# Offset convolution on whitened images in SBUF, with the row weights made pair by pair beside it

## What is computed

```python
x = _L0_conv_ref(x, L0_conv_beta)                  # X_hat = wm @ (x - mean) + beta
om = conv_general_dilated(x, w_off, padding=1) + b_off      # 27 planes: 9 y offsets, 9 x offsets, 9 mask logits
mask = sigmoid(om[:, 18:])
py = off_y + hs + ky ;  px = off_x + ws + kx       # where each of the 9 taps samples
sampled = bilinear(x, py, px) * mask
out = einsum("bckhw,ock->bohw", sampled, w) + b
out = relu(batch_norm(out)) + x
```

## Time and profile before

| what | us |
|---|---|
| median of three runs | 2315.51 |
| the profiled execution | 2317.37 |
| its span, first to last instruction | 2315.2 |
| busy PE / DVE / ACT / POOL | 1634.0 / 1592.1 / 1454.3 / 611.2 |
| last DMA issue of whitening | 191.77 |
| first instruction of offset convolution | 195.75 |
| first load of the row-weight stage | 348.71 |
| last store of the row-weight stage, issue | 649.82 |
| first instruction of the main loop's block | 669.19 |
| first sampling matmul | 697.82 |
| first load of the far-window stage | 2091.83 |

### The profile page before, as it was taken

How to read it: one execution, slowest core, us unless ns; L and a number is a source line. 1 busy time by engine, 2 the same in 40 slices (tenths; PEclk the granted TensorE clock), 3 DMA queues, 4 the chain that set the end, 5 groups by cost and what they waited for, 6 DMA issues and landing times. The chain is left out here.

```text
span 2315.2 us, 62313 instructions
## 1 busy us (share of the span) xinstructions
PE 1634.0 (71%) x24206; PEld 1092.1 (47%) x24207; DVE 1592.1 (69%) x2182; ACT 1454.3 (63%) x2219; POOL 611.2 (26%) x1168
## 2 busy tenths in 40 slices
PE   4756980000008999999999999999999999990620
PEld 4532330000006666666666666666666666660310
DVE  5343006656717898898898898998998899993205
ACT  2211224343217898898898898998998899980102
POOL 2000000000033444444444443434444444430000
PEclk9788995555557999999999999999999999995555
DMA  2177874667675766666667766666667666640008
GB/s 117 33 189 187 237 216 157 214 235 277 219 228 118 163 145 157 155 150 147 162 141 153 162 146 142 167 148 154 159 150 151 156 148 160 152 98 23 3 0 341
DMA packets 288863, 362.22 MB, mean 156 GB/s; under 512 B 61852, under 2 KB 260819, under 8 KB 285013
## 3 DMA queue, kind: packets, MB, share of 16 engines
q1 hardware_dynamic: 209552, 226.57, 38.8%
q0 software_dynamic: 36864, 59.94, 11.6%
q10 hardware_dynamic: 42182, 72.05, 9.1%
HBM read 253.94 MB, written 104.39 MB: 155 GB/s over the span
## 5 line engine op out<-in xcount | busy, mean ns | idle before, releaser
L758 POOL DMA_DIRECT2D rows<-scratch_parts x1152 | 587.5, 518 | 799.5 <-PE ps_even_y L790 777.3
L799 PE MATMUL ps_odd_y<-rows,sel 32*128 32x504 f32 (+2 forms) x928 | 465.3, 501 | 362.6 <-DMA rows<-scratch_parts 348.8
L942 DVE TENSOR_TENSOR G<-odd_y,ps_odd_v 128x504 f32<-128x504 f32 (+2 forms) x928 | 571.9, 658 | 127.7 <-PE ps_odd_v L820 85.7
L820 PE MATMUL ps_odd_v<-tent_x,stage 32*128 32x171 f32 (+1 forms) x5568 | 654.5, 329 | 0.0
L890 ACT COPY odd_y<-ps_odd_y 128x504 f32<-128x504 f32 (+2 forms) x928 | 527.7, 569 | 117.2 <-PE ps_odd_y L799 99.1
L820 PE MATMUL ps_even_v<-tent_x,stage 32*128 32x171 f32 (+3 forms) x5568 | 552.8, 329 | 37.8 <-ACT even_v L896 29.3
L951 DVE TENSOR_TENSOR G<-even_v,ps_even_y 128x1008 f32<-128x1008 f32 (+2 forms) x464 | 539.4, 1163 | 22.8 <-ACT even_v L896 22.6
L820 PEld LDWEIGHTS ps_odd_v<-tent_x,stage 32*128 32x128 f32 x5568 | 515.8, 189 | 0.0
L820 PEld LDWEIGHTS ps_even_v<-tent_x,stage 32*128 32x128 f32 x5568 | 429.2, 189 | 182.4 <-issue 168.7
L838 PE MATMUL ps_r<-G,conv_w 128*32 128x224 f32 (+1 forms) x8832 | 483.4, 346 | 9.8 <-ACT res L901 9.8
L896 ACT COPY even_v<-ps_even_v 128x1008 f32<-128x1008 f32 (+2 forms) x464 | 450.5, 971 | 23.5 <-PE ps_odd_v L820 15.8
(11 more groups left out here) (134 smaller groups left out, 951.8 us busy)
## 6 DMA issues: line engine op xcount, KB each, us to landing
place<-scratch_px SPq DMA_DIRECT2D x960, 105.0 KB, 3.5
scratch_parts<-parts ACTq DMA_DIRECT2D x18, 3136.0 KB, 16.9
rows<-scratch_parts POOLq DMA_DIRECT2D x960, 52.5 KB, 3.5
x<-scratch_xh SPq DMA_DIRECT2D x48, 406.0 KB, 6.3
place<-scratch_px SPq DMA_DIRECT2D x192, 84.0 KB, 2.9
scratch_om<-om ACTq DMA_DIRECT2D x64, 196.0 KB, 7.0
rows<-scratch_parts POOLq DMA_DIRECT2D x192, 42.0 KB, 2.8
scratch_conv<-res SPq DMA_DIRECT2D x448, 14.0 KB, 1.9
```

What stands on the lines that cost most here:

```text
L758: pool.dma_start(bass.AP(tensor=rows[b][:].tensor, offset=32 * g * pitch + here, ap=[[2 * pitch, Y_KINDS], [GROUP * W, 3], [1, count * W]] ...
L799: nc.tensor.matmul(ps_odd_y[:, lo:hi], sel[32 * g:32 * g + 32, :], taps(rows, 32 * g, 32, p, lo, hi), start=True, stop=True).then_inc(odd_ ...
L820: m = nc.tensor.matmul(sub(ps_v[g // 2], 0, 128, i * 512 + lo + first, dims), stage[32 * g:32 * g + 32, j * IMAGE + v * C:j * IMAGE + (v + ...
L942: nc.vector.tensor_tensor(sub(G, 0, 128, slot(v) + i * ROW + lo, [[1, hi - lo]]), odd_y[p % 3][:, i * ROW + lo:i * ROW + hi], ps_v[1][:, i ...
```

## The change

Blocks 3 and 4 become one block (L458 to L633 of the new kernel).

- `XH` stays in SBUF until that block ends, and the convolution reads it there. It works by groups of four pairs that stand side by side on the partitions. A chunk covers four pairs: 9 taps x 4 pairs x 2 halves of the image = 72 matmuls, each 32 rows x 64 columns on 392 points, into four PSUM banks, with two such sets (L548). A group has four chunks, and there are four groups. The loads of `x3` are gone, and the stores of `xh` remain for the residual.
- DVE takes the chunks out of PSUM, four pairs in one instruction of 1568 elements (L600), and adds a `pattern` that holds bias, tap shift and column, so that the x planes hold `px` at once. Ranges are taken per group over all planes, two reductions of 6272 elements (L608). `px` is no longer stored by itself.
- SP stores a group with 16 DMAs of 54 rows x 784 (L503). POOL loads a pair's logits and y offsets as 126 partitions x 448 (L528), two pairs ahead of their use, as soon as the pair that held the buffer has been multiplied.
- Row weights go by pair, 16 turns in place of 9: mask and eight distances (L563, L565), cap (L620), multiply (L623), round into `high` (L573), remainder into `tent_y` in place (L632). `high` has two buffers and `tent_y` three. ACT stores both with one DMA each (L578, L581).
- DVE takes the next group's chunks out between multiply and remainder in the first two pairs of a group, and its ranges in the third.
- Under this block SP loads the first `stage` (48 DMAs, at its start) and the first `place` (after group 0 is stored); POOL loads the first `rows` after pair 2. The clearing of `stage` and `rows` moves to the statistics block, the loads of `sel`, `conv_w`, `conv_b`, `at` to the start of whitening on ACT.
- The main loop's code stays but for its sources: `place` comes from `om`, whose planes (27 an image, 32 before) now lie in DRAM as their even rows and then their odd rows.
- The far-window stage reads two range tables with runs of 7 floats in place of four contiguous ones, and reduces them with 8 short instructions in place of 4 long.

The core of the diff (L458 of before goes, the new block comes; the pieces for the far windows are left out):

```diff
-                            sp.dma_start(sub(x3[b], dy * 2 * C, 2 * C, 0, [[1, H * PADW]]),
-                                         dram("xh", pair * 2 * C * PADHW + dy * PADW,
-                                              [[PADHW, 2 * C], [1, H * PADW]])).then_inc(x3_loaded[b], 16)
...
+                for c in range(len(BANDS)):
+                    load_stage(sp, 0, c)
+                for g in range(GROUPS):
+                    sp.wait_ge(evacuated, NCH * (g + 1))
+                    for q in range(PER_GROUP):
+                        for j in range(4):
+                            h, i = j // 2, j % 2
+                            sp.dma_start(dram("om", (g * GB + 2 * q + i) * OM_IMG + h * OM // 2,
+                                              [[HW, PLANES], [HW // 2, 2], [1, OM // 2]]),
+                                         sub(om, 32 * j, PLANES, q * OM, [[OM // 2, 2], [1, OM // 2]])).then_inc(om_stored, 16)
+                    if g == 0:
+                        sp.wait_ge(om_stored, 64 * PER_GROUP)
+                        load_place(sp, 0, 0)
...
+                    pool.wait_ge(om_stored, 64 * PER_GROUP * (pair // PER_GROUP + 1))
+                    wait(pool, distant, pair - 1)
+                    wait(pool, scaled, pair - 1)
+                    for tile, kind in ((mask[b], MASK), (oy[b], OY)):
+                        pool.dma_start(tile[:, :], dram("om", pair * 2 * OM_IMG + kind * KK * HW,
+                                                        [[OM_IMG, 2], [DCH, DENSE // 2], [1, DCH]])).then_inc(loaded[b], 16)
+                for pair in range(PAIRS):
+                    load_dense(pair)
+                    if pair == 2:
+                        pool.wait_ge(high_stored[0], 16)
+                        pool.wait_ge(low_stored[0], 16)
+                        load_rows(pool, 0, 0)
...
+                        wait(pe, evacuated, n - 1)
+                        top = ch // 2 + 2 * ROWS * (ch % 2)
+                        for k in range(KK):
+                            for q in range(PER_GROUP):
+                                for h in range(2):
+                                    m = nc.tensor.matmul(ps_o[n % 2][64 * h:64 * h + 64, q * 512:q * 512 + CH],
+                                                         woff[32 * q:32 * q + 32, k * 64:(k + 1) * 64],
+                                                         sub(XH, 32 * q, 32, g * PADHW + (h * HALF + top + k // 3) * PADW + k % 3,
+                                                             [[2 * PADW, ROWS], [1, W]]),
+                                                         start=(k == 0), stop=(k == KK - 1))
...
+                    act.wait_ge(loaded[b], 32 * (n // 2 + 1))
+                    wait(act, low_stored[n % 3], 16 * (n // 3))
+                    nc.scalar.activation(mask[b][:, :], mask[b][:, :], ACT.Sigmoid).then_inc(masked, 1)
+                    for r in range(WIN):
+                        a = nc.scalar.activation(tent_y[n % 3][:, r * DCH:(r + 1) * DCH], oy[b][:, :], ACT.Abs,
+                                                 bias=shift[0:DENSE, r:r + 1])
...
+                    where = [[DCH, DENSE], [B * KK * HW, WIN], [1, DCH]]
+                    act.wait_ge(high_ready, n + 1)
+                    act.dma_start(dram("parts", n * 2 * KK * HW, where), kinds(high[n % 2]).bitcast(fp32)
+                                  ).then_inc(high_stored[n % 2], 16)
+                    act.wait_ge(low_ready, n + 1)
+                    act.dma_start(dram("parts", (WIN * B + n * 2) * KK * HW, where), kinds(tent_y[n % 3])
+                                  ).then_inc(low_stored[n % 3], 16)
+                front(0)
+                for n in range(PAIRS):
+                    if n + 1 < PAIRS:
+                        front(n + 1)
+                    back(n)
+                    store(n)
...
+                    g, at = n // PER_GROUP + 1, n % PER_GROUP
+                    if g < GROUPS and at < 2:
+                        evacuate(g, 2 * at)
+                        evacuate(g, 2 * at + 1)
+                    if g < GROUPS and at == 2:
+                        take_ranges(g)
...
-                sp.wait_ge(cleared, 3)
-                load_place(0, 0)
-                load_place(0, 1)
-                for c in range(len(BANDS)):
-                    load_stage(0, c)
+                load_place(sp, 0, 1)
...
-                    sp.dma_start(sub(ranges, 0, PAIRS, k * n, [[1, n]]), dram(name, 0, [[n, PAIRS], [1, n]])).then_inc(S["x_ranges"], 16)
+                    sp.dma_start(sub(ranges, 0, PAIRS, k * 128 * HALF_UNITS, [[HALF_UNITS, 128], [1, HALF_UNITS]]),
+                                 dram(name, 0, [[HALF_UNITS, PAIRS], [PAIRS * HALF_UNITS, 128], [1, HALF_UNITS]])
+                                 ).then_inc(S["x_ranges"], 16)
```

More of the change, by code:

```diff
@@ L42 @@
 XT_ROW = XT_ROWS * C
-PLANE = B * KK * HW
-OM_IMG = 32 * HW
-DENSE = PLANE // 128
-DCH = 784
-CHUNKS = DENSE // DCH
-RANGES = ("oy_max", "oy_min", "ox_max", "ox_min")
+PX, OY, MASK = range(3)
+PLANES = 3 * KK
+OM_IMG = PLANES * HW
+DCH = 448
+DENSE = 2 * KK * HW // DCH
+RANGES = ("max", "min")
 NT = 10
@@ L115, in program @@
         wm = sb("wm", 128)
-        zeros = sb("zeros", XT_ROWS * C)
+        zeros = sb("zeros", NEAR * C)
+        IMAGE = VIEW_ROWS * C
+        sel32, sel = sb("sel32", 128), sb("sel", 128, f32r)
+        conv_w, conv_b, at = sb("conv_w", KK * 32), sb("conv_b", 1), sb("at", 1)
+        stage = sb("stage", len(COLUMNS) * IMAGE)
+        rows = [sb(f"rows{b}", KK * GROUP * W, f32r) for b in range(2)]
+        place = [sb("place0", KK * GROUP * W)]
+        dcn_loaded = sem("dcn_loaded")
+        BANDS = ((0, 16), (16, 16), (32, 16), (48, VIEW_ROWS - 48))
@@ L612, in program @@
             ROW = TAPS_PX
[L613 to L624 removed]
+            place.append(sb("place1", KK * GROUP * W))
             dist_x = [sb(f"dist_x{b}", ROW) for b in range(3)]
```

397 lines of the change are left out of this document (156 added, 241 removed).

## The result

The changed kernel took 2238.73 us (median of four runs, 2228.55 to 2248.60); the kernel before took 2313.91 beside it. The ratio is 0.9681, with a 95% interval of 0.963 to 0.9731. The gain is 75 us where 147 were forecast (2167, range 2135 to 2235): the sign was right, and the time lies 3.7 us beyond the range. The profiled execution took 2228.55 us, with a span of 2226.7.

What follows compares the result with a forecast made beforehand. It took the first two stages to be bound by a round trip of load, ACT, DVE and store, with no engine full. 2317.4 less 154.9 gained before the first sampling matmul, plus 4.4 of small terms, gave 2167 us, range 2135 to 2235.

Steps and rivals of the forecast that it cites:

- chunk of four pairs: Convolution: 72 matmuls, the eight of a tap side by side, 5.9 us; 11.9 if only four run abreast.
- group 0 out of PSUM: Start of the joint block: four chunks of 5.9 plus 2 from 200, then DVE's 1.8, done at 227.4.
- first plane load, issue to ACT's start: POOL's load of two tiles for the first pair: issues of about 1.35 and a landing of 3.5, 6.2 us.
- ten plain turns, mean: One pair's row weights: 14.6 us, ends 13.9 and 19.1; ACT and DVE in turn 13.9, buffers 14.5.
- turns of pairs 6 and 10, with ranges: Turns in which DVE also takes a group's ranges: 23.2 us, 8.6 more than a plain one.
- queue waits in the turns of pairs 2, 7 and 11: POOL's waits for plane stores: 3 us before pair 3's load, 4 each before pairs 4, 8 and 12; 15 us.
- last remainder to the block's end: Last weight stores of the joint block: issue 1.5 and 10.9 scaled to 3.61 MB, from 528.0 to 540.4.
- range tables: Far-window stage: 2 x 2048 runs of 28 bytes in place of four contiguous loads, 6 us lost, at most 17.6.
- the hand-over: Joint block to loop: clearing and first loads lie under the block, 2.5 us remain of 28.6.
- The first pair: Group 0's stores, 14.7 us, then the plane load, ACT and DVE work; the first remainder ends at 268.2.
- The first rival: Joint block's transfers spread over fewer DMA engines: slower stores or loads, 2197 to 2230, put at 2205; chance 0.25.
- The other rivals: Four matmuls abreast, 2220 (0.07); moved loads not hidden, 2193 (0.04); convolution matmuls one after the other, 2680 (0.04).

Runs made afterwards that it cites:

- kernel 11: Changed kernel with the first stage, place and rows loads put back at the start of the main loop; 2258.3 us.
- kernel 3: Changed kernel with POOL loading each tile of planes as two transfers of 63 rows, one per image; 2197.3 us.
- Kernel 12: Changed kernel storing only the first 112, 98 or 113 of each weight store's 126 rows, no issue added; 2210.0, 2207.8 and 4006.4 us.
- kernel 1: Changed kernel with each image's planes stored as 32 rows in place of 27; 2231.9 us.
- kernel 4: Changed kernel with one semaphore per pair of a group, so plane loads wait only for that pair's own stores; 2201.8 us.
- kernel 2: Changed kernel with the pairs' planes on 128 rows of 441 elements in place of 126 of 448; 2194.5 us.
- kernel 5: Changed kernel with the edits of kernel 2, kernel 3 and kernel 4 together; 2132.5 us.

## Why the prediction was right and wrong

Step by step, from the profiled execution:

| step | predicted | measured |
|---|---|---|
| first convolution matmul | 200 | 201.5 |
| chunk of four pairs | 5.9 | 5.98 |
| group 0 out of PSUM | 227.4 | 229.7 |
| its 16 stores landed | 242.1 | 247.1 |
| first plane load, issue to ACT's start | 6.2 | 13.5 |
| first remainder ends | 268.2 | 280.4 |
| ten plain turns, mean | 14.6 | 14.6 |
| turns of pairs 6 and 10, with ranges | 23.2 | 22.9 |
| queue waits in the turns of pairs 2, 7 and 11 | 15 | 69 |
| last remainder to the block's end | 12.4 | 14.1 |
| block's start to first sampling | 2.5 | 1.6 |
| first sampling matmul | 542.9 | 609.6 |
| loop | 1394 | 1393.8 |
| range tables: first load to reductions, before 5.6 | +6 | +4.5 |

The convolution, the instruction times scaled from the earlier trace rows, the hand-over and the assumption that nothing else moves were right. The 2 us that group 0's sum holds beside its four chunks is the author's estimate, and no run shows it as such; in the profiled execution the first chunk took 8.57 us from its first matmul to DVE's start (201.49 to 210.06), 2.6 more than the 5.98 of a later one, and the granted clock was 0.50 from 202 to 204, 0.52 from 204 to 206 and 1.00 from there. The plain turn came out right by luck in part. Five of the ten took 13.0 to 13.1, the bare round of ACT and DVE, put at 13.9 with 1.5 for an issue of the low store that took 0.32. The other five took 15.3 to 17.7, in which ACT waited for planes, put at 14.5. The two errors cancel in the mean. The miss of 66.7 us has two terms, and little else (12.2 + 53.7 + 1.7 - 0.9):

- **The queue waits, 54 us.** The step that failed is "I put 4 on each, between 0 and 8" for the group's stores, and 3 for pair 3. The three turns concerned took 39.5, 42.0 and 40.1 us; less 23.2 for pair 2's ranges and 14.6 for each other turn that leaves 69. The prediction gives no working for the 4 us. Its one price of a group's stores is that of group 0, an issue of 0.48, which is that of a load, and a landing of 7.0, of stores from one queue. Beside the weight stores an issue took 2.0 to 2.6 us, and the 16 with their landing 35 to 48. The trace before did have two queues storing at once: in each chunk SP stored `px` right behind ACT's two stores.

```profile
388.41 1.62 SPq L538 DMA_DIRECT2D scratch_px<-px  x2
```

```profile
scratch_px<-px SPq DMA_DIRECT2D x18, 196.0 KB, 6.0
```

That is 0.81 for an issue and 6.0 for a landing, so this row alone would not have told of the 2.0 to 2.6 either. The prediction named POOL as the engine that waits, but not that ACT would stand in pair n+1's mask with pair n's rounding queued behind it.
- **The first pair, 12 us.** The planes left PSUM 2.3 us late. The stores took 2.7 longer, at 0.88 per issue and not 0.48. The load took 7.3 longer: it was put at two issues of 1.35, which took 0.96 and 0.85, and a landing of 3.5, the price of a row load. Two things made it slow, and each of two edits took most of that away: 8.9 us with no `place` loads beside it (kernel 11), 6.7 beside them but with one load per image (kernel 3), in place of 13.5. The prediction put the moved `place` loads at nothing in the place they went to.

The first rival, transfers spread over fewer engines, came nearest. It had 0.25, a price of 2205 and an upper case of 2230, and 2238.7 was measured. Its mechanism is there. Kernel 12 shows it for the weight stores. For the loads the landings of kernel 3 point to it (3.0 us with 63 rows as the outermost dimension, 10.0 with two images), and so does POOL's queue in kernel 11 from 250 to 254, where four loads of two images ran alone:

```profile
q0 software_dynamic: 583, 0.63, 50.3%
```

That is 8 of 16 engines for four loads, or two for each if no two loads share one, an estimate: no row shows a load alone. But the rival did not act as it was costed. It expected turns of 16 or more and waits for `high` or `low` stores; plain turns had a mean of 14.6, ACT waited for no store, and the loss sits in three turns. For the 27-row plane stores, kernel 1 found no gain from 32 rows. Nor does the rival hold the loss that kernel 4 took away, which is that a pair waits for the whole group's stores. The forecast left the row counts to that rival; those of the weight stores alone are worth some 31 us (kernel 12; 35 in kernel 2 with what else it changes). The range's upper end, 2235, lay 5 us above the rival's upper case, with no room for the wait of a whole group beside it.

The other rivals are out: eight matmuls run abreast (5.98 us a chunk), the moved loads hide from the loop (kernel 11), and no convolution matmul waited for another.

What stays open is why SP's issues stretch. With 113 rows, where ACT's stores trickle over one engine, SP issued its 16 in 16.8 to 18.6 us although stores were nearly always under way; with half the weights they took 22 to 28, with all of them 32 to 41. So it goes with the weight traffic beside them and not with the mere presence of a backlog. While group 2's stores were issued, the DMA engines, at 0.84, were not far from the 89.2% that the weight stores reach alone:

```profile
376.00:412.00 36.00, 11.30 (x264) 5.18 (x248) 31.77 (x8) 8.11 (x10) 0.00 (x0) 0.69 0.84 246
```

That the two share the time of the engines fits this, but no run shows it: kernel 1's stores, on 15.3 engines in place of 8.6 by their shares alone, were issued no faster (42.29 us for group 2's 16 against 40.89). How the losses of kernels 2, 3 and 4 (35, 32 and 35 us) divide among the waits was not separated either; together they gave 106, their sum of 102 within the scatter of "first" (609.6 and 614.8 for the same kernel), and more than the forecast had hoped for: kernel 5's first sampling matmul comes 40 us before the 542.9 of the prediction.

## What to carry to other kernels

Before costing a transfer, look at the outermost dimension on both sides. Stores of 126 rows ran on 14 engines here, of 112 and 128 on 16, and of 113 on one, and a load whose DRAM side begins with two images landed in 10.0 us where one of 63 rows took 3.0. The 126 rows and the two images cost 30 to 35 us each, and the edits that cured them are a line and five lines. For a store that will run beside another stream keep an end of the range for several times the lone price. Even a row with two streams can miss it: SP's two `px` stores behind ACT's took 0.81 each, the 16 plane stores 2.0 to 2.6. And where a load waits for a batch of stores, let each consumer wait for its own stores: whoever works in order behind it (ACT here) holds up finished work as well.

## What the runs showed of the hardware beyond that

One row more than 112 put a store on one engine (6.4% of 16): 128 us a pair, where an undisturbed turn with 112 rows took 13.0, and a kernel of 4006 us. While that engine still carried the store before, the *issue* on ACT lasted 55 to 72 us, so ACT's own work stopped, not only its data. Cutting a store in two can cost more than it spreads: in undisturbed turns two issues in a row for a low half took ACT 3.7 to 4.0 us where one took 0.32. And the loop of some 1395 us came out between 1388 and 1405 from kernel to kernel, kernel 11 aside, and at 1393.8 and 1400.9 for the same kernel.
